# Expert stage of an adaLN mixer block: units of 512 tokens in place of tiles of 256

## What is computed

```python
h = layernorm(x) * (1 + ca) + sa                      # modulation from silu(c) @ wmod
x = x + ga * attn(h)                                  # conv, state space scan, projection: 4 x 512 tokens
h = layernorm(x) * (1 + cb) + sb
x = x + gb * ffn(h)
# ffn, for x_flat (2048, 512), two experts, hidden width 2048
logits = x_flat @ w_router.T
probs = softmax(logits)
top_idx = argmax(probs); top_weight = probs[top_idx]
h = einsum('nd,ehd->enh', x_flat, w_fc)
a = square(where(h >= 0, h, 0.5 * h))
expert_out = einsum('enh,edh->end', a, w_proj)
out = einsum('end,en->nd', expert_out, mask * top_weight)   # one expert for each token
```

## Time and profile before

| what | value |
|---|---|
| median of 3 runs | 620.27 us (619.74 to 624.72) |
| profiled execution, span from first to last instruction | 626.6 us |
| profiled execution, time around the span | not given by the page |
| PE busy | 545.7 us, 87% |
| VectorE, ScalarE, GpSimd busy | 394.7, 282.3, 209.2 us |
| chain that ended last: fc products (L912), proj products (L940) | 32%, 28% of the span |
| mean granted TensorE clock | 0.936 of full speed |

### The profile page before, as it was taken

The page is one execution under the profiler, slowest core; times in us unless marked ns, Lnnn a source line. Parts: engine busy times, 40 slices in busy tenths (PEclk is TensorE's granted clock), DMA queues, the critical chain, the costliest instruction groups (busy, mean ns, idle before and its releaser), DMA issues.

```text
span 626.6 us, 11028 instructions
## 1 busy us (share of the span) xinstructions
PE 545.7 (87%) x3052; PEld 441.0 (70%) x3052; DVE 394.7 (63%) x801; ACT 282.3 (45%) x679; POOL 209.2 (33%) x185
## 2 busy tenths in 40 slices
PE   5989959494528899999999999999999999998860
PEld 0435444453327899999999999999999999987750
DVE  3697889898893565454555545555545455567862
ACT  2668583532114455454445445455445445432320
POOL 1030276684886121122122122122112212157541
PEclk9999969789658999999999999999999999999996
DMA  8911543030267520201201202202101010077641
GB/s 314 390 69 52 217 152 120 0 137 1 84 235 236 222 69 2 70 16 51 69 0 67 67 0 67 67 0 67 64 3 67 6 61 0 0 242 245 182 143 67
DMA packets 17042, 61.40 MB, mean 98 GB/s; under 512 B 3051, under 2 KB 3051, under 8 KB 13688
## 3 DMA queue, kind: packets, MB, share of 16 engines
q1 hardware_dynamic: 11256, 42.63, 19.3%
q0 software_dynamic: 5760, 18.43, 8.2%
HBM read 47.30 MB, written 14.27 MB: 98 GB/s over the span
## 4 chain that ended last, share of the span: by engine, by line
PE 71%; DVE 11%; issue 8%; ACT 3%; DMA 2%; another core or an unknown queue 2%; POOL 1%; DVEq 0%; SPq 0%; ACTq 0%; POOLq 0%
PE bank L912 32%; PE bank L940 28%; PE bank L756 3%; DVE xc L1076 3%; PE bank L821 2%; DVE junk L1151 1%; PE bank L774 1%; PE bank L789 1%; PE bank L826 1%; DVE u L1089 1%; DMA sorted_tokens<-gap,gapI 1%; DVE st L1019 1%; DMA wm<-wmod 1%; DVE res L1126 1%
## 5 line engine op out<-in xcount | busy, mean ns | idle before, releaser
L490 POOL TENSOR_TENSOR Wlo<-raw,Whi (+1 forms) x64 | 82.3, 1290 | 276.4 <-ACT Whi L651 276.3
L912 PE MATMUL bank<-XShi,Whi 128*128 (+1 forms) x576 | 165.7, 288 | 5.7 <-DVE twice_h L1341 4.9
L912 PE MATMUL bank<-XShi,Wlo 128*128 (+1 forms) x576 | 164.1, 285 | 0.0
L912 PE MATMUL bank<-XSlo,Whi 128*128 (+1 forms) x576 | 164.1, 285 | 0.0
L1360 DVE TENSOR_TENSOR acc<-acc,bank 128x512 f32 (+1 forms) x126 | 85.9, 687 | 71.7 <-PE bank L940 66.6
L1341 DVE TENSOR_TENSOR twice_h<-relu_h,bank 128x256 f32<-128x256 f32 x144 | 60.2, 420 | 99.4 <-ACT relu_h L713 96.8
L912 PEld LDWEIGHTS bank<-XShi,Whi 128*128 128x128 f32 x576 | 111.6, 194 | 12.1 <-issue 9.8
L940 PE MATMUL bank<-Whi,ahi 128*128 128x512 f32 x272 | 107.9, 397 | 6.6 <-DVE alo L1349 6.5
L912 PEld LDWEIGHTS bank<-XSlo,Whi 128*128 128x128 f32 x576 | 111.6, 194 | 2.1
L912 PEld LDWEIGHTS bank<-XShi,Wlo 128*128 128x128 f32 x576 | 111.5, 194 | 0.0
L940 PE MATMUL bank<-Wlo,ahi 128*128 128x512 f32 x272 | 107.3, 394 | 0.0
(11 more groups left out here) (146 smaller groups left out, 605.9 us busy)
## 6 DMA issues: line engine op xcount, KB each, us to landing
raw<-wffn SPq DMA_DIRECT2D x16, 1024.0 KB, 5.2
wm<-wmod SPq DMA_DIRECT2D x6, 1024.0 KB, 12.4
res_row<-sorted_residuals SPq DMA_DIRECT2D x18, 260.0 KB
sorted_rows<-sorted_tokens SPq DMA_DIRECT2D x9, 512.0 KB, 10.8
x_in<-x SPq DMA_DIRECT2D x4, 1024.0 KB, 10.1
bc<-mod_rows SPq DMA_DIRECT2D x4, 772.0 KB, 7.0
ga_bc<-ga_rows SPq DMA_DIRECT2D x4, 256.0 KB, 3.5
wx_sb<-wx SPq DMA_DIRECT2D x1, 514.0 KB, 10.7
```

Of the source, the lines that this page charges most:

```text
L490: pool.tensor_tensor(Wlo[:, hb % 2, c, :], raw[:, c, :], Whi[:, hb % 2, c, :].bitcast(F32), ALU.subtract).then_inc(s_wlo, 1)
L912: mm = pe.matmul(hP[m][:, 0:TILE], W[wp][:, par, 2 * e + k // 2, o:o + P], XS[xp][:, k, bass.ds(t * TILE, TILE)], start=(n == 0), stop=(n ...
```

## The change

Tiles are paired. A unit u is 512 rows (`UNIT`), tiles 2u and 2u + 1; there are NU = 5 units, the last of which is one tile. fc writes 512 columns of `hP[m]` with one product in place of two. Where the border between the experts falls between the two tiles of a unit, both halves are computed apart (`mixed`). relu writes `twice_h` itself, twice adds `hP[m]` to it in place, `a_full` lies in PSUM banks 6 and 7, and `ahi`, `alo` and `twice_h` hold a whole unit. `s_au` is gone: `ahi` and `alo` are written again when proj of the whole unit before is done. proj goes piece by piece: wait for the bank, all six products of the piece, signal. The orders become fc(u), proj of unit u - 1 (four pieces), and on VectorE twice(u), accumulate of two tiles, low(u), in the last block followed by finish_rows of two tiles. In block 0, proj of unit 0 comes before fc(1), the transposes of unit u + 1 come behind fc(u), and ScalarE copies them ahead of the squares of unit u. Two chunks of weights are split after each of units 0 to 3. `sct` and `back` share one buffer, and `u` of the mixer is called `eabs`.

```diff
+UNIT = 2 * TILE
+NU = (NT + 1) // 2
...
-        alo = at("alo", [P, HM, TILE], F32R, o_a)
-        ahi = at("ahi", [P, HM, TILE], F32R, o_a + AB)
-        relu_h = at("relu_h", [P, HM, TILE], F32, o_a + 2 * AB)
-        twice_h = at("twice_h", [P, HM, TILE], F32, o_a + 3 * AB)
-        a_full = at("a_full", [P, HM, TILE], F32, o_a + 4 * AB)
+        alo = at("alo", [P, HM, UNIT], F32R, o_a)
+        ahi = at("ahi", [P, HM, UNIT], F32R, o_a + AB)
+        twice_h = at("twice_h", [P, HM, UNIT], F32, o_a + 2 * AB)
...
+        a_full = bank[6:8]
...
-        s_au = [sem("a_used0"), s_yy[SUB - 1]]
...
+        def tiles_of(u):
+            return range(2 * u, min(2 * u + 2, NT))
+        def columns_of(u):
+            return TILE * len(tiles_of(u))
+        def splits_after(u):
+            return (2 * u, 2 * u + 1) if u < NU - 1 else ()
...
+            def relu(hb, u):
+                i, n = NU * hb + u, columns_of(u)
                 for m in range(HM):
                     act.wait_ge(s_h[m], i + 1)
-                    wait(act, s_q[m], i)
-                    act.activation(relu_h[:, m, :], hP[m][:, 0:TILE], ACT.Relu).then_inc(s_relu[m], 1)
+                    wait(act, s_ah[m], i)
+                    wait(act, s_af[m], i)
+                    act.activation(twice_h[:, m, 0:n], hP[m][:, 0:n], ACT.Relu).then_inc(s_relu[m], 1)
+            def squares(hb, u):
+                i, n = NU * hb + u, columns_of(u)
                 for m in range(HM):
                     act.wait_ge(s_q[m], i + 1)
-                    wait(act, s_au[m], i)
-                    act.activation(ahi[:, m, :], twice_h[:, m, :], ACT.Square, scale=0.5).then_inc(s_ah[m], 1)
+                    wait(act, s_yy[SUB - 1], NT * hb + 2 * u)
+                    act.activation(ahi[:, m, 0:n], twice_h[:, m, 0:n], ACT.Square, scale=0.5).then_inc(s_ah[m], 1)
                     wait(act, s_al2[m], i)
-                    act.activation(a_full[:, m, :], twice_h[:, m, :], ACT.Square, scale=0.5).then_inc(s_af[m], 1)
+                    act.activation(a_full[m][:, 0:n], twice_h[:, m, 0:n], ACT.Square, scale=0.5).then_inc(s_af[m], 1)
...
+            for u in range(NU):
+                relu(0, u)
+                if u < NU - 1:
+                    for t in tiles_of(u + 1):
+                        high_rows(t)
+                squares(0, u)
...
             with act.Fori(1, NHB - 1) as hb:
+                for u in range(NU):
+                    relu(hb, u)
+                    squares(hb, u)
+                    if u == 0:
+                        act.wait_ge(s_yy[SUB - 1], NT * hb)
+                    for c in splits_after(u):
+                        act.wait_ge(s_raw[c // 4], 16 * (hb + 2))
                         split(hb + 1, c)
-            with act.Fori(0, NT) as t:
-                job(NHB - 1, t)
+            for u in range(NU):
+                relu(NHB - 1, u)
+                squares(NHB - 1, u)
...
-            def fc(par, hb, t):
+            def fc(par, hb, u, wide):
+                i = NU * hb + u
+                def products(m, e, first, count):
+                    n = 0
+                    for k in range(KT):
+                        for wp, xp in PARTS:
+                            o = HB * (k % 2) + P * m
+                            mm = pe.matmul(hP[m][:, first:first + count], W[wp][:, par, 2 * e + k // 2, o:o + P],
+                                           XS[xp][:, k, bass.ds(u * UNIT + first, count)],
+                                           start=(n == 0), stop=(n == 3 * KT - 1))
+                            n += 1
+                    return mm
+                def body(e, count):
                     for m in range(HM):
+                        products(m, e, 0, count).then_inc(s_h[m], 1)
+                def mixed():
+                    for m in range(HM):
+                        products(m, 0, 0, TILE)
+                        products(m, 1, TILE, TILE).then_inc(s_h[m], 1)
                 for m in range(HM):
                     wait(pe, s_q[m], i)
+                if wide:
+                    with pe.If(n0 > u * UNIT + TILE):
+                        body(0, UNIT)
+                    with pe.Else():
+                        with pe.If(n0 > u * UNIT):
+                            mixed()
+                        with pe.Else():
+                            body(1, UNIT)
+                else:
+                    with pe.If(n0 > u * UNIT):
+                        body(0, TILE)
+                    with pe.Else():
+                        body(1, TILE)
...
+            def proj(par, hb, u, half):
+                t = 2 * u + half
                 i = NT * hb + t
                 def body(e, subs):
+                    for s in range(SUB):
+                        o = TILE * half + P * s
+                        wait(pe, s_yu[s], i)
+                        if s not in subs:
+                            mm = pe.matmul(yP[s][:, :], ahi[:, 0, o:o + P], Whi[:, par, 4 + 2 * e, :], start=True, stop=True)
+                        else:
+                            for m in range(HM):
+                                for n, (ap, wp) in enumerate(PARTS):
+                                    mm = pe.matmul(yP[s][:, :], A[ap][:, m, o:o + P], W[wp][:, par, 4 + 2 * e + m, :],
+                                                   start=(m == 0 and n == 0), stop=(m == HM - 1 and n == 2))
+                        mm.then_inc(s_yy[s], 1)
...
+            def proj_unit(par, hb, u, halves):
+                for m in range(HM):
+                    pe.wait_ge(s_al2[m], NU * hb + u + 1)
+                for half in range(halves):
+                    proj(par, hb, u, half)
...
             def rest_of_block(par, hb, last=False):
+                fc(par, hb, 1, True)
                 proj_weights_ready(hb)
+                proj_unit(par, hb, 0, 2)
+                with pe.Fori(2, NU - 1) as u:
+                    fc(par, hb, u, True)
+                    proj_unit(par, hb, u - 1, 2)
+                fc(par, hb, NU - 1, False)
+                proj_unit(par, hb, NU - 2, 2)
                 if not last:
                     fc_weights_ready(hb + 1)
+                    fc(1 - par, hb + 1, 0, True)
+                proj_unit(par, hb, NU - 1, 1)
...
+            for u in range(NU):
+                pe.wait_ge(s_xhi, SUB * (tiles_of(u)[-1] + 1))
+                pe.wait_ge(s_xlo, SUB * (tiles_of(u)[-1] + 1))
+                fc(0, 0, u, u < NU - 1)
+                if u < NU - 1:
+                    for t in tiles_of(u + 1):
+                        transpose_rows(t)
+                if u == 0:
                     proj_weights_ready(0)
+                if u > 1:
+                    proj_unit(0, 0, u - 1, 2)
+                if u < 1:
+                    proj_unit(0, 0, u, 2)
...
+            for u in range(NU):
+                twice(0, u)
+                if u < NU - 1:
+                    for t in tiles_of(u + 1):
+                        low_rows(t)
+                if u > 1:
+                    for t in tiles_of(u - 1):
+                        accumulate("first", 0, t)
+                low(0, u)
+                if u < 1:
+                    for t in tiles_of(u):
+                        accumulate("first", 0, t)
...
+            for u in range(1, NU):
+                twice(NHB - 1, u)
+                for t in tiles_of(u - 1):
+                    accumulate("add", NHB - 1, t)
+                low(NHB - 1, u)
+                for t in tiles_of(u - 1):
+                    finish_rows(t)
             accumulate("add", NHB - 1, NT - 1)
             finish_rows(NT - 1)
```

More of the change, by code:

```diff
@@ L100, in build @@
         o_acc = o_xs + 2 * XSB
-        AB = HM * TILE * 4
+        AB = HM * UNIT * 4
         o_a = o_acc + NT * SUB * DM * 4
-        o_const = o_a + 5 * AB
+        o_const = o_a + 3 * AB
         raw = at("raw", [P, CH, 512], F32, o_raw)
@@ L132, in build @@
         x_in = take("x_in", [P, XRING, TJ, DM])
-        u = take("u", [P, L])
+        eabs = take("eabs", [P, L])
         w1 = take("w1", [P, L])
@@ L219, in build @@
         back = const("back", [P, NB * TJ])
+        sct = back
         n0f = const("n0f", [P, 1])
@@ L918, in fc @@
                 for m in range(HM):
                     wait(pe, s_q[m], i)
-                with pe.If(n0 > t * TILE):
-                    body(0)
-                with pe.Else():
-                    body(1)
-            def proj(par, hb, t):
+                if wide:
[11 more added lines that the diff above has]
+                        body(1, TILE)
@@ L946, in proj @@
-                for m in range(HM):
-                    pe.wait_ge(s_al2[m], i + 1)
-                for s in range(SUB):
-                    wait(pe, s_yu[s], i)
+                    for s in range(SUB):
[9 more added lines that the diff above has]
+                        mm.then_inc(s_yy[s], 1)
@@ L1374, in finish_rows @@
                     dve.tensor_tensor(sub, sub, row[:, 0:DM], ALU.add).then_inc(s_or[s], 1)
```

(48 more changed lines are left out.)

96 lines of the change are left out of this document (16 added, 80 removed).

## The result

The changed kernel takes 643.06 us (median of 4 runs, 641.99 to 647.21), the kernel before in the same session 622.5 (4 runs). The ratio is 1.0365, 95% interval 1.0313 to 1.0417: **3.7% slower**. Ratios leave out executions more than 1.5% above the fastest of their kernel, and they are not the quotients of the medians beside them (here 1.033). The forecast was 641.0 in 624 to 655. Its profiled execution has a span of 640.2 us, 13.6 more than that of before. But its mixer happened to finish 4.5 us sooner, so the spans alone mislead. I cut every execution at three marks: the start of the last scatter of gap rows by GpSimd; the moment when block 1 has two fc tiles done and block 0 is finished (before 256.93, after 265.49); and the same point of block 7 (554.38, 565.25), the last block.

What follows compares the result with a forecast made beforehand. TensorE alone was taken to bound the middle blocks, running dry at both ends. Start +13.2, middle +3.1 and last block +4.2 gave +20.5 us: span 647, median 641 us, range 624 to 655.

Steps and rivals of the forecast that it cites:

- The merge: Wide fc: two 256-column products become one of 512, saving 0.0100 us each, 0.96 us a block, 7.7 over 8 blocks.
- Stalls one and two: Middle blocks: TensorE waits for accumulate before proj(2)'s third piece, and for alo before proj(3), 0.8 us each.
- the old stall of 0.13: Old block: an fc of 3.01 us in place of 2.87, forecast to go, -0.13 us a block.
- The middle: Blocks 1 to 6: savings and new stalls sum to +0.5 us a block, +3.1 us in all.
- Start: Block 0 up to fc(1,0) and proj(0,8) done: 270.3 in place of 257.1, +13.2 us, ends +6 and +17.
- ScalarE's late copy: Block 0: ScalarE's second copy, 1.6 us late before, is late again; proj(0) starts at 207.7.
- The half clock: Start: TensorE at 1.2 GHz costs 1.5 us once before proj(0), half a time after fc(1): 2.3 us.
- The wait behind fc(1): Block 0: TensorE restarts 5.4 us after fc(1), transposes fill 1.8, so a 3.6 us stall.
- Last block: Block 7: VectorE without a pause, TensorE waiting; +0.2 from the order and +4 more, +4.2 us in all.
- late signals and half clock: Last block: late signals falling on squares, and half clock after gaps of 2 to 3 us: +4, from 0 to 9.
- Rival 5: TensorE's longer loop list no longer fits, and three passes pay for code streaming: +10.5 us, 652 us; chance 0.12.
- rival 4: Last block: late signals belong to ScalarE's rolled loop and vanish written out, -14 instead of +4.2, 609 us; chance 0.09.

Runs made afterwards that it cites:

- run 4: The changed kernel without TensorE's branch for a unit in which both experts have tokens: 645.55 us, ratio 1.034 to the kernel before.
- run 5: The changed kernel with fc products of 256 columns again and without the branch for a mixed unit: 662.47 us, ratio 1.0671 to the kernel before.
- Run 6: The changed kernel with block 0 reordered, squares of unit 0 ahead of rows of tiles 2 and 3, proj(0) cut in halves: 632.75 us, ratio 1.0164.
- run 1: The changed kernel with fc products two of 256 columns again in place of one of 512: 674.59 us, ratio 1.0794 to the kernel before.
- the three together: The changed kernel with the start order of Run 6, full-precision squares first and four banks for proj: 622.89 us, ratio 1.0032 to the kernel before.

## Why the prediction was right

**The merge** was mis-sized: 0.96 us a block forecast, 1.35 measured (runs 4 and 5). I took 0.2292 us for a product of 512 columns from proj. That is a mean: in the kernel before the first six products of a proj, behind a narrow fc, start 0.232 us apart and the other six 0.2267, and 0.2267 is what a wide fc takes. So a pair saves 0.0125, 1.20 a block, and most of the other 0.15 is that a proj behind a wide fc has no slow first half. The Trainium skill's formula for an isolated product ("TensorE: Matmul & The Clock Gate", "Back-to-back issue gap") would have given 0.2 a block and is further off: the rows show some 13 ns over the columns' time at either width.

**Stalls one and two** were forecast at 0.8 each; taking them away brought 0.83 and 0.87. Both were where the sum put them, but made up otherwise. At the first, TensorE restarts 0.05 us behind the accumulate and not 0.27, so the hole is 0.58 us, and slow first products add 0.15. At the second the restart is 0.79, not 0.61: proj(3) starts 3.88 us behind the end of proj(2), not 3.71. And the old stall of 0.13, which the sum let go, comes back at the narrow fc: even with both stalls taken away, fc(4) takes 2.99 to 3.01 us for 2.87 and proj(3) 5.57 for 5.44, 0.26 in all. From start to start a block is 49.58 - 0.14 (the old stall) - 1.46 (1.20 in fc, 0.26 in proj) + 0.26 + 0.73 + 0.87 = 49.84, as undisturbed blocks show; the mean of all is 49.96. Forecast 50.1. The middle is +2.3, not +3.1: the products save more than I put down, and that outweighs the 0.26 and the longer restart, which I left out.

**Start**, +13.2 forecast, +13.1 measured, where executions differ by up to 3.4: a sum right by two errors, and in that by luck. ScalarE's late copy, which I carried over from one execution, didn't come again, and proj(0) began at 205.4 on the clock of before, not 207.7. The half clock cost 5.1 us and not 2.3: proj(0) ran at it for 14 of its 24 products (until 206.6), and fc(2) in part. The wait behind fc(1) came as forecast, 5.5 us from its end to fc(2) where I had 5.4. Run 6 and those with its order show that the order is the cause of 6 to 8 of the 13; what the rest is made of no run takes apart.

**Last block**, +4.2 forecast, +2.8 measured (0.9 and 3.4 with the last blocks of runs 4 and 6, which are the same code), by a partly wrong mechanism. I had VectorE without a pause and TensorE waiting. TensorE waits, but VectorE is idle for 17 of 63 us, since it waits for TensorE in turn. Of the +4 that I put for late signals and half clock, the signals did not come: no wait there has a remote releaser. The clock did fall, to 0.86, 0.83 and 0.71 in the stretches from 600 us on; before it had 0.83 and 0.79 in two of six. GpSimd stayed hidden until VectorE's last operation.

**Rival 5**, the list that doesn't fit, holds in its traffic (46 packets in place of 16) and not in its price: a hole of 0.3 us at one loop turn (365.3 us) instead of 3.5 at each. The price exists, and starts a little further on: 57 packets cost 6.4 us a pass (run 1). The Trainium skill, "Runtime: NRT & Kernel Launch", "Instruction fetch mechanics", says that a taken branch out of the fetched window stalls until its page has come. The changed kernel's loop fetches again in every pass (10 or 11 packets), and 0.3 us is the most that it shows; the trace agrees only from run 1's list on (13 or 14 packets). Of rival 4 the condition came about and the price did not: with ScalarE's last block written out there is no remote wait, and the block is still longer than before. Nor is the rolled loop shown to be their cause, since runs 1 and 5, just as written out, have such waits again.

## What to carry over

Larger units save a little in every instruction and cost where something has one buffer: ask, for every buffer that grows with the unit, what follows the wait for its release and how long the shortest cover is, and put in front of that wait whatever does not need it (two lines here, 0.9 us a block). A unit that doubles also doubles what must be there before the first product: the start cost 13 us, and still 5 to 7 with a better order, most of what the middle gave with both stalls gone (7.9). And count an unrolled loop body in fetch packets: growing a list until it is fetched anew in each pass cost next to nothing here, and the next growth 6 us a pass.

## What the hardware showed that I had not expected

A ScalarE operation of 512 columns that writes PSUM took 0.58 us in the changed kernel and 0.60 in the three together, one that writes SBUF 0.60 to 0.64. With nothing else changed, a longer TensorE list (13 or 14 fetch packets in a pass in place of 11) stopped it for 3.8 and 4.1 us at a DMA share of 0.02, while lists with 46 packets in all stopped it for 0.3 to 0.6. While indirect gathers ran in a burst, ScalarE and VectorE together went on only 3.9 us after the product that they had waited for (560.19 to 564.06), and ScalarE in the kernel before 7 us (562.3 to 569.28).
